# Combining the experts' rows: centring on ScalarE, gamma and residual by batch, the next batch's rows in between

## The chip, the cores and the metric

The kernel runs on one core of a Trainium2 chip. The metric is the device time of one execution in microseconds. A core has TensorE (matrix products, PE in the rows), VectorE (DVE), ScalarE (ACT), GpSimd (POOL) and SyncE (SP), each with its own instruction queue that it works off in the order in which it is written; they synchronise through semaphores. A queue that waits for a semaphore starts nothing that stands behind the wait.

## The reference

Two layers of gated attention and feed-forward over x of 8 x 512 x 256 float32. The stage in question is the end of the first feed-forward (a mixture of experts, each token goes to its two best) and the beginning of the second attention. Cut to that:

```python
combined = jnp.sum(gates[..., None] * ybuf[pos], axis=1)
res = hidden_states + combined.reshape(B, S, D)
mu = jnp.mean(res, -1, keepdims=True)
var = jnp.var(res, -1, keepdims=True)
ffn = (res - mu) * jax.lax.rsqrt(var + 1e-05) * ln_gamma + ln_beta
x = x + jnp.tanh(g_ffn[0]) * ffn                        # end of layer 0
q = _layernorm(x) @ q_map                               # layer 1, attention
k, v = ctx_1024 @ k_map, ctx_1024 @ v_map
```

There are B = 8 batches of 512 tokens. A batch lies on 128 partitions as TPB = 4 tiles of 128 tokens by 256 features.

## The kernel before

The program is a row of stages: projection, attention 0, routing, placing, experts, combining, attention 1, merging, quantised output. The change is in the function `combine`. Its engines run over the eight batches, each by a queue written out by hand, and the order below is the one in which each engine meets its work.

VectorE, batch b (the loop of `@block.vector`): it adds the two experts' rows, times their gates, into the batch's accumulator `acc`, which is a part of `S.BIG` (8 instructions of 128x256, line 2035); takes the statistics of `acc` (`nb1.stats`, line 233 and 237); subtracts the mean and multiplies by gamma (4 instructions, line 2042); multiplies by the reciprocal deviation and adds x (4 instructions, line 2047); takes the statistics of the new x (`nb2.stats`); cuts the low part of batch b's keys (`k1.cut_low`, line 460); and cuts the low part of the queries of the batch before (`low_queries(b - 1)`, line 2025). That last one opens with

```python
e.wait_ge(q_high, b + 1)
```

so `low_queries(b - 1)` waits until ScalarE has evicted the high part of the queries of batch b - 1.

GpSimd raises the variances to the power -1/2 for both norms (line 242 and 245), makes `shift`, minus the mean times the reciprocal deviation, for the second norm (lines 2014 and 2016), and issues the loads of expert rows (`load_rows`) and of the context. ScalarE evicts every product from PSUM and writes the normalised x into `hn` (`normalise`, 4 instructions, line 2149), as soon as `shift` is there.

TensorE runs in rounds. Round b is: turn `hn` of batch b (line 1226, into `c_pH`), keys of batch b + 1 (line 1943 into `c_pK`), queries of batch b (line 1943 into `c_pQ`), turn the context of batch b + 2 (`c_pC`), values of batch b + 1 (line 1233). Round b can't begin before ScalarE has written all four tiles of `hn` of batch b. After the last round the first maxima of attention 1 are taken (`ahead`, line 345 on TensorE and line 351 on VectorE).

Of the kernel before, what the change touches and what calls it, by code (L numbers as in the profile page):

```python
# [11 lines left out]
ALU = mybir.AluOpType  # L12
# [1206 lines left out]
def tiles(b):  # L1219
    return ds(b * TPB, TPB)  # L1220
# [732 lines left out]
def combine(S):  # L1953
# [4 lines left out]
    with ctx:  # L1958
# [5 lines left out]
        nb1, nb2 = Norm(S, sb, sem, "1", 1), Norm(S, sb, sem, "2", 2)  # L1964
        product, shift = ([sb(f"{x}{j}", [P, TPB]) for j in range(2)] for x in ("product", "shift"))
        shifted = sem("shifted")
        q1 = [inputs.query_parts(j) for j in range(2)]
        k1 = Projection(sem, "k1", S.ks[1], sb("full_k1", [P, KD, SEQ]), [inputs.key_parts(j) for j in range(2)], inputs.stored_k)
        cT = [sb(f"cT{j}", [P, KD, SEQ]) for j in range(2)]
# [13 lines left out]
        with nc.Block() as block:  # L1983
            @block.gpsimd
            def _(e):
                def load_rows(b):
                    if b >= 2:
                        e.wait_ge(added, (b - 1) * ADDS)
                    for kk in range(2):
                        first = E * CAP + kk * N + b * SEQ  # L1990
                        e.dma_start(yg[b % 2][:, kk, :, :], S.ytok[first:first + SEQ, :].rearrange("(t p) d -> p t d", p=P)
                                    ).then_inc(got[b % 2][kk], 16)

                def load_context(b):
                    e.wait_ge(turned_c, b)
                    e.dma_start(context[:, :, :], S.a["ctx_1024"][b, :, :].rearrange("(t p) c -> p t c", p=P)
                                ).then_inc(ld_c, 16)

                e.wait_ge(S.yst, 16 * E * NCH * TILES)
                load_rows(0)  # L2000
                load_context(1)
                load_rows(1)
                values.count_column(e).then_inc(counted, 1)
                inputs.clear(e, range(last))
                for i in range(B):
                    if i == B - 1:
                        e.wait_ge(added, (B - 1) * ADDS)
                        inputs.clear(e, (last,))
                    nb1.power(e, i, 0)
                    if i + 2 < B:  # L2010
                        load_rows(i + 2)
                    nb2.power(e, i, i % 2)
                    e.wait_ge(nb2.powed, i + 1)
                    e.tensor_tensor(product[i % 2][:, :], nb2.mv[i % 2][:, :, 0], nb2.rstd[i % 2][:, :], ALU.mult).then_inc(shifted, 1)
                    e.wait_ge(shifted, 2 * i + 1)
                    e.tensor_scalar(shift[i % 2][:, :], product[i % 2][:, :], -1.0, None, ALU.mult).then_inc(shifted, 1)
                    if i + 2 < B:
                        load_context(i + 2)

            @block.vector  # L2020
            def _(e):
                def low_queries(b):
                    hi, lo = q1[b % 2]
                    e.wait_ge(q_high, b + 1)
                    e.scalar_tensor_tensor(out=lo, in0=pQ[:, :, :], scalar=0.25, in1=hi,
                                           op0=ALU.mult, op1=ALU.subtract).then_inc(q_low, 1)

                for w, src in ((wk1, "wk1"), (wq1, "wq1")):
                    e.tensor_copy(dims_first(w[:, :, :], True), dims_first(S.w[src][:, :, :], False)).then_inc(ordered, 1)
                for b in range(B):  # L2030
                    x, acc = S.X[:, tiles(b), :], S.BIG[:, tiles(b), :]
                    for kk in range(2):
                        e.wait_ge(got[b % 2][kk], 16 * (b // 2 + 1))
                        for t in range(TPB):
                            e.scalar_tensor_tensor(out=acc[:, t, :], in0=yg[b % 2][:, kk, t, :],
                                                   scalar=S.gate[:, kk, ds(b * TPB + t, 1)], in1=acc[:, t, :],
                                                   op0=ALU.mult, op1=ALU.add).then_inc(added, 1)
                        e.wait_ge(added, b * ADDS + (kk + 1) * TPB)
                    nb1.stats(e, b, 0, acc)
                    e.wait_ge(nb1.agg, (b + 1) * TPB)  # L2040
                    for t in range(TPB):
                        e.scalar_tensor_tensor(out=acc[:, t, :], in0=acc[:, t, :], scalar=nb1.mv[0][:, t, 0:1],
                                               in1=S.w["gamma_b"][:, :], op0=ALU.subtract, op1=ALU.mult).then_inc(centred, 1)
                    e.wait_ge(centred, (b + 1) * TPB)
                    e.wait_ge(nb1.powed, b + 1)
                    for t in range(TPB):
                        e.scalar_tensor_tensor(out=x[:, t, :], in0=acc[:, t, :], scalar=nb1.rstd[0][:, t:t + 1], in1=x[:, t, :],
                                               op0=ALU.mult, op1=ALU.add).then_inc(upd, 1)
                    e.wait_ge(upd, (b + 1) * TPB)
                    if b >= 2:  # L2050
                        e.wait_ge(nb2.normed, (b - 1) * TPB)
                    nb2.stats(e, b, b % 2, x)
                    k1.cut_low(e, b)
                    if b:
                        low_queries(b - 1)
                for m in range(6):
                    ahead.take(e, m)
                low_queries(B - 1)
                for m in range(6, AHEAD):
                    ahead.take(e, m)  # L2060
                    if m == UNITS - 1:
                        ahead.turn(e)
# [63 lines left out]
            def _(e):  # L2126
# [17 lines left out]
                def normalise(b):  # L2144
# [3 lines left out]
                    for t in range(TPB):  # L2148
                        e.activation(hn[:, t, :], S.X[:, b * TPB + t, :], ACT.Identity, bias=shift[b % 2][:, t:t + 1],
                                     scale=nb2.rstd[b % 2][:, t:t + 1]).then_inc(nb2.normed, 1)  # L2150

                def take_turned(b):
                    e.wait_ge(trh, b + 1)
                    if b:
                        e.wait_ge(q_done, b)
                    e.activation(hT[:, :, :], pH[:, :, :], ACT.Copy).then_inc(hte, 1)
# [8 lines left out]
                take_keys(0)  # L2165
                take_context(1)
                take_values(0)
                normalise(0)
                for b in range(B):
                    take_turned(b)  # L2170
                    if b + 1 < B:
                        take_keys(b + 1)
                    high_queries(b)
                    if b + 2 < B:
                        take_context(b + 2)
                    if b + 2 == B:
                        take_values(b + 1)
                        normalise(b + 1)
                    elif b + 1 < B:
                        normalise(b + 1)  # L2180
                        take_values(b + 1)
# [329 lines left out]
```

## Time and profile before

| | |
|---|---|
| time, median of 3 executions | 1591.46 us (1590.18 to 1594.08) |
| the profiled execution's own time | 1592.47 us |
| its span in the profile | 1590.7 us |
| TensorE busy over the span | 1462.8 us, 92% |
| VectorE busy | 1242.2 us, 78% |
| ScalarE busy | 1020.7 us, 64% |
| GpSimd busy | 662.2 us, 42% |
| combining, from its first instruction to the next stage | 1038.8 to 1177 us |

The span runs from the first to the last instruction that the profiler recorded; the 1.8 us by which the execution's own time is longer lie around it. Times in the rows are microseconds from the start of the span, durations follow the start, and the text in square brackets is how long the engine stood idle before a row and what released it. PEclk is the granted clock of TensorE as a share of full speed: 1.00 is 2.4 GHz, 0.50 is 1.2 GHz.

### The profile page before, as it was taken

To read this page: it belongs to the slowest core of one execution; us is meant where nothing else is said; L and a number is where in the kernel's file an instruction comes from. 1 tells how busy PE (TensorE), PEld (TensorE's weight loads), DVE (VectorE), ACT (ScalarE), POOL (GpSimd) and SP (SyncE) were. 2 spreads that over 40 slices of the span, in tenths; PEclk is the share of its full clock that TensorE was granted. 3 is DMA by queue.
4 is the path that set the end of the run, shared out by engine and by line. 5 is a ranking of instruction groups with operands and counts; after the bars stand their busy time and mean duration, and the time that the engine had idled before them with its cause. 6 is when DMAs were issued, how large, how long until landed. Compare 5 with 4: busy or idle time off the path is not lost. (4 is left out here: it accounts for less than half of the span.)

```text
span 1590.7 us, 29625 instructions
## 1 busy us (share of the span) xinstructions
PE 1462.8 (92%) x11054; PEld 957.8 (60%) x11054; DVE 1242.2 (78%) x1873; ACT 1020.7 (64%) x1761; POOL 662.2 (42%) x1081
## 2 busy tenths in 40 slices
PE   7989999999998599999999999869979999999976
PEld 6863333333387499999999999735523333333455
DVE  6889999999665766666665564369979999999696
ACT  5648999998934444444444444335549998989736
POOL 4315666666222333443442432254415555555030
PEclk9989999999996699999999999979979999999998
DMA  9974444444273222222222221158844444444103
GB/s 287 333 222 103 129 129 129 129 128 129 67 276 108 63 65 85 80 77 90 77 83 87 77 80 38 43 184 283 251 112 125 128 129 128 129 127 129 49 0 107
DMA packets 118749, 198.65 MB, mean 125 GB/s; under 512 B 29568, under 2 KB 63680, under 8 KB 117584
## 3 DMA queue, kind: packets, MB, share of 16 engines
q1 hardware_dynamic: 83840, 111.22, 22.4%
q0 software_dynamic: 33360, 83.94, 18.4%
q8 instruction: 89, 1.46, 0.4%
q10 hardware_dynamic: 1408, 1.61, 0.3%
q14 instruction: 52, 0.43, 0.1%
HBM read 117.77 MB, written 77.87 MB: 123 GB/s over the span
## 5 line engine op out<-in xcount | busy, mean ns | idle before, releaser
L1156 ACT ACTIVATE i_room<-a_ring 128x512 f32<-128x512 f32 x1024 | 547.4, 608 | 57.7 <-PE a_ring L1092 11.3
L351 DVE TENSOR_REDUCE logit<-a_ring 128x2 f32<-128x1024 f32 x416 | 499.7, 1223 | 18.4 <-PE a_ring L345 15.4
L1103 PE MATMUL a_pout<-i_room,values 128*17 128x256 f32 x4096 | 309.1, 386 | 3.3 <-ACT i_room L1156 1.8
L1862 ACT ACTIVATE e_full<-e_pH,b1T 128x320 f32<-128x320 f32 x256 | 135.1, 528 | 245.4 <-PE e_pH L1803 234.7
L1811 PE MATMUL e_pY<-fc_w,e_hid_hi 128*128 128x512 f32 x640 | 237.1, 407 | 0.6 <-DVE e_hid_lo L1917 0.6
L1092 PE MATMUL a_ring<-i_qk 64*128 64x512 f32 x768 | 189.8, 491 | 1.5 <-DVE logit L351 1.4
L1646 POOL DMA_INDIRECT w<-normed,slot_get x80 | 84.0, 1050 | 231.8 <-PE fc_turned L1788 195.6
L1812 PE MATMUL e_pY<-fc_w,e_hid_lo 128*128 128x256 f32 x640 | 179.8, 281 | 0.0
L1103 PEld LDWEIGHTS a_pout<-i_room,values 128*17 128x17 f32 x4096 | 74.6, 95 | 170.5 <-ACT i_room L1156 137.3
L1092 PEld LDWEIGHTS a_ring<-i_qk 64*128 64x128 f32 x768 | 72.5, 186 | 154.5 <-DVE logit L351 110.0
L345 PE MATMUL a_ring<-i_qk 64*128 64x512 f32 x712 | 149.1, 415 | 17.2 <-ACT i_room L1156 12.5
L1917 DVE TENSOR_TENSOR e_hid_lo<-e_full,e_hid_hi 128x640 fp32r<-128x640 f32 x128 | 118.3, 924 | 58.8 <-ACT e_hid_hi L1871 58.8
L1803 PE MATMUL e_pH<-e_rowsT_hi,fc_w1T_hi 128*128 128x320 f32 x512 | 159.7, 312 | 0.8 <-DVE e_rowsT_lo L1726 0.8
L1803 PE MATMUL e_pH<-e_rowsT_lo,fc_w1T_hi 128*128 128x320 f32 x512 | 159.1, 311 | 0.0
L1803 PE MATMUL e_pH<-e_rowsT_hi,fc_w1T_lo 128*128 128x320 f32 x512 | 158.4, 309 | 0.0
L1811 PEld LDWEIGHTS e_pY<-fc_w,e_hid_hi 128*128 128x128 f32 x640 | 120.3, 188 | 24.3 <-DVE e_hid_lo L1917 0.9
L1935 POOL DMA_INDIRECT ytok<-e_y,slot_put x80 | 82.7, 1034 | 93.2 <-DVE e_y L1895 78.6
L1812 PEld LDWEIGHTS e_pY<-fc_w,e_hid_lo 128*128 128x128 f32 x640 | 121.3, 189 | 0.0
L1871 ACT ACTIVATE e_hid_hi<-e_full 128x640 fp32r<-128x640 f32 x128 | 94.7, 740 | 11.9 <-ACT e_full L1862 0.4
L1803 PEld LDWEIGHTS e_pH<-e_rowsT_hi,fc_w1T_hi 128*128 128x128 f32 x512 | 96.8, 189 | 6.7 <-issue 1.1
L1803 PEld LDWEIGHTS e_pH<-e_rowsT_lo,fc_w1T_hi 128*128 128x128 f32 x512 | 97.0, 189 | 0.0
L1803 PEld LDWEIGHTS e_pH<-e_rowsT_hi,fc_w1T_lo 128*128 128x128 f32 x512 | 96.9, 189 | 0.0
(360 smaller groups left out, 2510.1 us busy)
## 6 DMA issues: line engine op xcount, KB each, us to landing
ks<-i_room SPq DMA_DIRECT2D x64, 256.0 KB, 4.0
outs<-a_osb SPq DMA_DIRECT2D x64, 256.0 KB, 3.0
qs<-i_room SPq DMA_DIRECT2D x60, 256.0 KB, 4.4
fc_raw<-in_L_ffn_fc_w SPq DMA_DIRECT2D x15, 1024.0 KB, 5.3
i_qk<-ks POOLq DMA_DIRECT2D x84, 128.0 KB, 3.1
i_qk<-qs POOLq DMA_DIRECT2D x84, 128.0 KB, 3.2
BIG<-outs SPq DMA_DIRECT2D x64, 128.0 KB
ytok<-r_zeros SPq DMA_DIRECT2D x8, 1024.0 KB, 9.8
```

Source lines behind the costliest of these rows:

```text
L345: mm = e.matmul(banks[hh], q[at, p, t * P:(t + 1) * P], k[at, p, :], start=True, stop=True)
L351: return e.tensor_reduce(nmax[:, :].rearrange("p (x y t) -> p x y t", x=2, y=2)[:, :, p, t], pair[:, :, :], AX.X, ALU.max, negate=True)
L1092: mm = e.matmul(score_bank(n * U + i, hh), k[j][at, p, t * P:(t + 1) * P], q[j][at, p, :], start=True, stop=True)
L1103: mm = e.matmul(pout[32 * h:32 * h + VW, at], v[:, b * TPB + t, g * HG + h, :], pexp[t][:, h, at], start=(t == 0 and half == 0), stop=(t = ...
L1156: e.activation(pexp[t][:, 2 * p + hh, :], score_bank(n * U + i, hh), ACT.Exp).then_inc(exped, 1)
L1646: e.indirect_dma_start(expert_rows(S)[:, t, :], None, S.normed[:, :], bass.IndirectOffsetOnAxis(ap=S.slot_get[:, c:c + 1], axis=0)).then_i ...
L1803: mm = e.matmul(pH[h][:, 0:WIDE], w1T[x][pl][:, k, f * P:(f + 1) * P], rowsT[j][pr][:, k, h * WIDE:(h + 1) * WIDE], start=(k == 0 and n_pa ...
L1811: e.matmul(pY[t][:, :, :], hid[s % 3][HI][:, token], w2[x][:, f, :, :], start=(f == 0), stop=False)
L1812: mm = e.matmul(pY[t][:, HI, :], hid[s % 3][LO][:, token], w2[x][:, f, HI, :], start=False, stop=(f == KF - 1))
L1862: e.activation(full[s % 2][:, h * WIDE:(h + 1) * WIDE], pH[h][:, 0:WIDE], ACT.Silu, bias=S.b1T[:, n * KF + f:n * KF + f + 1]).then_inc(act, 1)
L1871: e.activation(hid[s % 3][HI][:, :], full[s % 2][:, :], ACT.Copy).then_inc(hi, 1)
L1917: e.tensor_tensor(hid[s % 3][LO][:, :], full[s % 2][:, :], hid[s % 3][HI][:, :], ALU.subtract).then_inc(lo, 1)
```

## The change

Four things change, all in `combine`. First, VectorE's four instructions that subtract the mean and times gamma, and the four that scale and add x, go. Second, ScalarE gets `centre(b)`, four activations that turn `acc` into (acc - mean) times the reciprocal deviation, with a second `shift1` that GpSimd makes in two more small instructions per batch. Third, VectorE multiplies by gamma and adds to x in one instruction of 128x1024 each. Fourth, VectorE's order changes: after the statistics of `acc`, it cuts the low keys, cuts the low queries of the batch before, and adds the next batch's expert rows (`add_rows(b + 1)`); only then it waits for `centre(b)` and goes on with gamma, x and the statistics of x.

```diff
+        product1, shift1, shifted1 = sb("product3", [P, TPB]), sb("shift3", [P, TPB]), sem("shifted1")
@@ gpsimd
                     nb1.power(e, i, 0)
+                    e.wait_ge(nb1.powed, i + 1)
+                    e.tensor_tensor(product1[:, :], nb1.mv[0][:, :, 0], nb1.rstd[0][:, :], ALU.mult).then_inc(shifted1, 1)
+                    e.wait_ge(shifted1, 2 * i + 1)
+                    e.tensor_scalar(shift1[:, :], product1[:, :], -1.0, None, ALU.mult).then_inc(shifted1, 1)
                     if i + 2 < B:
                         load_rows(i + 2)
@@ vector
-                for b in range(B):
-                    x, acc = S.X[:, tiles(b), :], S.BIG[:, tiles(b), :]
+                def add_rows(b):
+                    acc = S.BIG[:, tiles(b), :]
...
+                add_rows(0)
+                for b in range(B):
+                    x, acc = S.X[:, tiles(b), :], S.BIG[:, tiles(b), :]
+                    if b:
+                        e.wait_ge(centred, b * TPB)
                     nb1.stats(e, b, 0, acc)
-                    e.wait_ge(nb1.agg, (b + 1) * TPB)
-                    for t in range(TPB):
-                        e.scalar_tensor_tensor(out=acc[:, t, :], in0=acc[:, t, :], scalar=nb1.mv[0][:, t, 0:1],
-                                               in1=S.w["gamma_b"][:, :], op0=ALU.subtract, op1=ALU.mult).then_inc(centred, 1)
+                    k1.cut_low(e, b)
+                    if b:
+                        low_queries(b - 1)
+                    if b + 1 < B:
+                        add_rows(b + 1)
                     e.wait_ge(centred, (b + 1) * TPB)
-                    e.wait_ge(nb1.powed, b + 1)
-                    for t in range(TPB):
-                        e.scalar_tensor_tensor(out=x[:, t, :], in0=acc[:, t, :], scalar=nb1.rstd[0][:, t:t + 1], in1=x[:, t, :],
-                                               op0=ALU.mult, op1=ALU.add).then_inc(upd, 1)
-                    e.wait_ge(upd, (b + 1) * TPB)
+                    e.tensor_tensor(acc, acc, over_tiles(S.w["gamma_b"]), ALU.mult).then_inc(upd, 1)
+                    e.wait_ge(upd, 2 * b + 1)
+                    e.tensor_tensor(x, x, acc, ALU.add).then_inc(upd, 1)
+                    e.wait_ge(upd, 2 * b + 2)
                     if b >= 2:
                         e.wait_ge(nb2.normed, (b - 1) * TPB)
                     nb2.stats(e, b, b % 2, x)
-                    k1.cut_low(e, b)
-                    if b:
-                        low_queries(b - 1)
@@ scalar
+                def centre(b):
+                    acc = S.BIG[:, tiles(b), :]
+                    e.wait_ge(shifted1, 2 * b + 2)
+                    for t in range(TPB):
+                        e.activation(acc[:, t, :], acc[:, t, :], ACT.Identity, bias=shift1[:, t:t + 1],
+                                     scale=nb1.rstd[0][:, t:t + 1]).then_inc(centred, 1)
...
                 take_values(0)
+                centre(0)
                 normalise(0)
...
                     if b + 2 < B:
                         take_context(b + 2)
+                    if b + 1 < B:
+                        centre(b + 1)
```

VectorE's queue for one batch in the middle of the stage, before. `BIG` is the accumulator, `c_yg` the expert rows, `c_full_k` the keys, `c_pQ` the queries:

```order
L2035 SCALAR_TENSOR_TENSOR BIG<-c_yg,gate,BIG 128x256 x8
L233 BN_STATS c_stats<-BIG 128x6 x4
L237 BN_AGGR c_mv<-c_stats 128x2 x4
L2042 SCALAR_TENSOR_TENSOR BIG<-BIG,c_mv,gamma_b 128x256 x4
L2047 SCALAR_TENSOR_TENSOR X<-BIG,c_rstd,X 128x256 x4
L233 BN_STATS c_stats<-X 128x6 x4
L237 BN_AGGR c_mv<-c_stats 128x2 x4
L460 TENSOR_TENSOR i_room<-c_full_k,i_room 128x1024
L2025 SCALAR_TENSOR_TENSOR i_room<-c_pQ,i_room 128x1024
```

The same batch's loop body on VectorE in the changed kernel:

```order
L233 BN_STATS c_stats<-BIG 128x6 x4
L237 BN_AGGR c_mv<-c_stats 128x2 x4
L460 TENSOR_TENSOR i_room<-c_full_k,i_room 128x1024
L2030 SCALAR_TENSOR_TENSOR i_room<-c_pQ,i_room 128x1024
L2040 SCALAR_TENSOR_TENSOR BIG<-c_yg,gate,BIG 128x256 x8
L2057 TENSOR_TENSOR BIG<-BIG,gamma_b 128x1024
L2059 TENSOR_TENSOR X<-X,BIG 128x1024
L233 BN_STATS c_stats<-X 128x6 x4
L237 BN_AGGR c_mv<-c_stats 128x2 x4
```

The two rows that cut the low keys and the low queries stood behind the statistics of X; they now stand ahead of them, and the addition of expert rows (of the next batch now) stands between.

ScalarE's queue for one round in the changed kernel, from the eviction of the turned `hn` to that of the next batch's values:

```order
L2171 ACTIVATE c_hT<-c_pH 128x1024
L2145 ACTIVATE c_full_k<-c_pK 128x1024
L455 ACTIVATE i_room<-c_full_k 128x1024
L2177 ACTIVATE i_room<-c_pQ 128x1024
L2139 ACTIVATE c_cT<-c_pC 128x1024
L2164 ACTIVATE BIG<-BIG,c_shift,c_rstd 128x256 x4
L2157 ACTIVATE c_hn<-X,c_shift,c_rstd 128x256 x4
L2150 ACTIVATE values<-c_pK 128x64x16
```

Before, the row L2164 wasn't there, and the others stood in this order.

## Rows read from the trace of the kernel before

**Rows 1.** Windows of the combining stage: per engine busy us (instructions), PEclk, DMA share, GB/s.

```profile
1060.20:1157.00 96.80, 89.84 (x332) 54.81 (x332) 85.41 (x230) 55.18 (x69) 42.88 (x59) 0.97 0.80 256
1101.81:1115.48 13.67, 12.44 (x48) 7.68 (x49) 13.24 (x37) 8.03 (x11) 6.77 (x9) 1.00 0.94 304
```

**Rows 2.** Timeline, VectorE: start, duration, line, operation [idle before].

```profile
1086.04 3.37 DVE L2035 SCALAR_TENSOR_TENSOR BIG<-c_yg,gate,BIG 128x256 f32<-128x256 f32 x8
...
1098.37 1.23 DVE L2025 SCALAR_TENSOR_TENSOR i_room<-c_pQ,i_room 128x1024 fp32r<-128x1024 f32 x1 [0.54 <-ACT i_room L2162]
1099.51 3.37 DVE L2035 SCALAR_TENSOR_TENSOR BIG<-i_qk,gate,BIG 128x256 f32<-128x256 f32 x8
...
1104.77 1.67 DVE L2042 SCALAR_TENSOR_TENSOR BIG<-BIG,c_mv,gamma_b 128x256 f32<-128x256 f32 x4
...
1108.37 1.41 DVE L233 BATCH_NORM_STATS2 c_stats<-X 128x6 f32<-128x256 f32 x4
...
1110.11 1.19 DVE L460 TENSOR_TENSOR i_room<-c_full_k,i_room 128x1024 fp32r<-128x1024 f32 x1
...
1112.35 3.37 DVE L2035 SCALAR_TENSOR_TENSOR BIG<-c_yg,gate,BIG 128x256 f32<-128x256 f32 x8
```

**Rows 3.** Timeline, TensorE, one round and the next round's start.

```profile
1101.81 1.09 PE L1226 MATMUL c_pH<-ident,c_hn 128*128 128x128 f32 x8 [0.21 <-ACT c_hn L2149]
1102.81 3.67 PE L1943 MATMUL c_pK<-c_cT,w 128*128 128x512 f32 x8
1106.32 3.60 PE L1943 MATMUL c_pQ<-c_hT,w 128*128 128x512 f32 x8
...
1110.63 3.62 PE L1233 MATMUL c_pK<-wv,c_cT 128*128 128x256 f32 x16
1115.48 1.09 PE L1226 MATMUL c_pH<-ident,c_hn 128*128 128x128 f32 x8 [1.23 <-ACT c_hn L2149]
```

**Rows 4.** Timelines, TensorE, ScalarE and VectorE, first round of the stage.

```profile
1060.18 1.97 PE L1226 MATMUL c_pH<-ident,c_hn 128*128 128x128 f32 x8 [7.05 <-ACT c_hn L2149]
1061.94 5.59 PE L1943 MATMUL c_pK<-c_cT,w 128*128 128x512 f32 x8
1067.37 3.60 PE L1943 MATMUL c_pQ<-c_hT,w 128*128 128x512 f32 x8
...
1071.01 1.02 ACT L2162 ACTIVATE i_room<-c_pQ 128x1024 fp32r<-128x1024 f32 x1 [1.32 <-PE c_pQ L1943]
...
1072.06 1.22 DVE L2025 SCALAR_TENSOR_TENSOR i_room<-c_pQ,i_room 128x1024 fp32r<-128x1024 f32 x1 [1.12 <-ACT i_room L2162]
1073.20 3.37 DVE L2035 SCALAR_TENSOR_TENSOR BIG<-i_qk,gate,BIG 128x256 f32<-128x256 f32 x8
1076.61 1.40 DVE L233 BATCH_NORM_STATS2 c_stats<-BIG 128x6 f32<-128x256 f32 x4
```

**Rows 5.** Windows of 1 us at a fall and a rise of the clock (PEclk).

```profile
1055.00:1056.00 1.00, 0.00 (x0) 0.00 (x0) 1.00 (x2) 0.00 (x0) 0.92 (x2) 0.85 1.04 389
...
1065.00:1066.00 1.00, 1.00 (x2) 0.34 (x1) 1.00 (x4) 0.00 (x0) 0.00 (x0) 0.53 0.96 283
```

**Rows 6.** Timelines, VectorE, GpSimd, ScalarE: statistics of x to its normalising, batch 3.

```profile
1094.90 1.41 DVE L233 BATCH_NORM_STATS2 c_stats<-X 128x6 f32<-128x256 f32 x4
...
1099.40 0.25 POOL L2016 TENSOR_SCALAR c_shift<-c_product 128x4 f32<-128x4 f32 x1
...
1099.68 2.08 ACT L2149 ACTIVATE c_hn<-X,c_shift,c_rstd 128x256 f32<-128x256 f32 x4 [0.43 <-POOL c_shift L2016]
```

**Rows 7.** Timelines, VectorE and ScalarE, batch 0 at the stage's start.

```profile
1052.90 1.40 DVE L233 BATCH_NORM_STATS2 c_stats<-X 128x6 f32<-128x256 f32 x4
...
1053.17 1.02 ACT L2142 ACTIVATE values<-c_pK 128x1024 f32<-128x1024 f32 x1 [2.43 <-PE c_pK L1233]
```

**Rows 8.** Timelines, TensorE and ScalarE, the last round of the stage.

```profile
1157.05 1.09 PE L1226 MATMUL c_pH<-ident,c_hn 128*128 128x128 f32 x8 [1.46 <-ACT c_hn L2149]
...
1164.96 1.02 ACT L2162 ACTIVATE i_room<-c_pQ 128x1024 fp32r<-128x1024 f32 x1 [5.76 <-PE c_pQ L1943]
```

## The prediction, made before the changed kernel ran

> **What bounds the kernel now.** I read the page of the profile first, then the windows of the combining stage, then the timelines of its engines, and last the windows of 1 us for the clock. From 1060.20 to 1157.00 us TensorE is busy for 89.84 of 96.80 us and VectorE for 85.41: both are nearly full, ScalarE (55.18) and GpSimd (42.88) are not [rows 1]. What sets the pace is VectorE. Its addition of expert rows for batches 3 and 5 starts at 1086.04 and 1112.35, so a batch takes (1112.35 - 1086.04) / 2 = 13.15 us; the only idle time is 0.54 us every other batch, when the low cut of the queries waits for ScalarE [rows 2]. TensorE follows: round 4 runs from 1101.81 to 1110.63 + 3.62 = 1114.25, which is 12.44 us of work without a gap, and then it waits 1.23 us for ScalarE's normalised rows [rows 3]. So by throughput there is 13.15 - 12.44 = 0.7 us a batch to be had, about 5 us over seven batches.
>
> **What is removed.** From the start of line 2042 to the start of the statistics of x, VectorE spends 1108.37 - 1104.77 = 3.60 us [rows 2]. In its place stand two instructions of 128x1024. The nearest row is the low cut of the keys, the same operation on the same shape from SBUF, 1.19 us [rows 2]; with some 0.05 us for the semaphore between dependent instructions I take 1.24 us each, 2.48 us together. Bounds: not below 1.19 each, since half the work can't be left out of that form; not above what four instructions of 256 took, 3.60 / 2 = 1.80 each. VectorE's own work falls by about 1.1 us a batch. On GpSimd the two more instructions cost about 0.25 us each by the row of `shift` [rows 6] and lie in time in which it waits. ScalarE gets four more activations, 2.08 us a batch by the row of the same shape [rows 6]; it has the room.
>
> **What is moved, and what then waits.** This part decides. The low cut of the queries of batch b - 1 stood behind the statistics of x of batch b; it now stands ahead of them. The low cut of the keys of b has moved with it, and those keys too are made in round b - 1, behind the turn. The queue is in order, so gamma, the residual and the statistics of x(b) can't start before ScalarE has evicted the queries of b - 1. Those queries need round b - 1 of TensorE, round b - 1 needs `hn` of b - 1, and this needs the statistics of x(b - 1). Before, x(b) was computed while round b - 1 ran. Now every batch is one closed chain: statistics of x, GpSimd's power and shift, normalise, turn, keys, queries, eviction, low cut, next rows, gamma, residual, statistics of x. I add it up from one start of turning `hn` to the next.
>
> 1. Turn to the end of the queries. In round 4 this took 1106.32 + 3.60 - 1101.81 = 8.11 us, at full clock [rows 3]. In round 0, where TensorE had been idle for 7.05 us before, it took 1067.37 + 3.60 - 1060.18 = 10.79 us, because turning took 1.97 instead of 1.09 us and the keys 5.59 instead of 3.67 [rows 4]. The clock row says why: with no matmul running the granted clock leaves 1.00 between 1055 and 1056 (0.85 in that microsecond) and stays at 0.50, which is 1.2 GHz, until it rises at the end of the microsecond from 1065 (0.53), well inside the keys [rows 5]. In the changed kernel TensorE's work of a round (12.44 us, or 2.68 more at the lower clock, 15.1) ends some 10 us before the next round can start, which is longer than those 7.05 us. So every round is like round 0, and I take 10.79.
> 2. End of the queries (1070.97) over the eviction (1071.01) and the low cut (1072.06) to the start of adding rows (1073.20): 2.23 us [rows 4]. In round 0 VectorE was free and waiting, as it will be.
> 3. Adding the next batch's rows: 1076.61 - 1073.20 = 3.41 us [rows 4].
> 4. Gamma and residual: 2.48 us, from above.
> 5. Statistics of x to the next turn: 1101.81 - 1094.90 = 6.91 us for batch 3 (GpSimd's shift at 1099.40, normalise at 1099.68) [rows 3, 6], and 1115.48 - 1108.37 = 7.11 us for batch 4 [rows 2, 3]. Mean 7.01.
>
> Sum: 10.79 + 2.23 + 3.41 + 2.48 + 7.01 = 25.92 us a batch, against 13.15.
>
> Is `centre(b + 1)` ready in time? ScalarE reaches it after evicting the queries and the context. The eviction of queries starts 0.04 us after they end and takes 1.02 us [rows 4], the context's as long, and the centring 2.08: ready 0.04 + 1.02 + 1.02 + 2.08 = 4.16 us after the end of the queries. VectorE comes to it 2.23 + 3.41 = 5.64 us after. It is hidden by 1.5 us; without that cover (no rows added, as in the last batch) it costs what is left over. There no context is evicted either: centring is ready after 0.04 + 1.02 + 2.08 = 3.14 us, against VectorE's 2.23, so this step costs 25.92 - 3.41 + 0.91 = 23.42 us.
>
> A rule of the Trainium skill is to be weighed here. The page "TensorE: Matmul & The Clock Gate", in "Part 1: The HAM clock gate", says that the ramp penalty is below 1% of a typical span and that a model shouldn't be fitted to a specific cold count. By it the ramp would be left out of step 1, which gives the time of the second rival below. The row of round 0 speaks against leaving it out, since here the ramp comes back in every round [rows 4].
>
> **The start.** Before, the statistics of x(0) start at 1052.90 and ScalarE evicts the values from 1053.17 to 1054.19 [rows 7]. After it stands `centre(0)`, 2.08 us, to 1056.3. VectorE has batch 0's weighted sum at 1052.90 - 3.60 - 1.85 = 1047.45 (1.85 us for the statistics of the accumulator is 1104.77 - 1099.51 - 3.41 [rows 2, 4]); statistics, low keys and the rows of batch 1 take 1.85 + 1.19 + 3.41 us more, to about 1054, so ScalarE ends last. Gamma and residual bring the statistics of x(0) to 1056.3 + 2.48 = 1058.8, 5.9 us later than before, and the first turn from 1060.18 [rows 4] to 1066.1.
>
> **The sum.** The turn of round 7 comes at 1066.1 + 6 x 25.92 + 23.42 = 1245.0 us; before it was at 1157.05 [rows 8]: 87.9 us later. From there to the eviction of the last queries it took 1164.96 - 1157.05 = 7.91 us [rows 8], with the turn at full clock. Now the clock is low from the start: 0.9 us for the turn and some 0.4 for what follows, 1.3 together. The rest of the stage is VectorE's row of maxima, unchanged. So + 89.2 us: 1592.47 + 89.2 = 1681.7 for an execution like the profiled one, and 1.0 less, as it lay 1.0 above the median: 1680.7, **1681 us**, 5.6% slower.
>
> **Rivals.**
> - *Clock stays low longer, and the queries run at 1.2 GHz too.* They would take 3.60 x 5.59 / 3.67 = 5.48 us, 1.9 more in each of seven rounds: 1681 + 13 = 1694. For it: TensorE's share of busy time falls to about a half. Against: in round 0 the same pause and the same work had the clock back before the queries [rows 4, 5]. 6 in 100.
> - *No loss by the clock.* Rounds 1 to 6 take 2.68 less each, the tail 1.3: 1681 - 17 = 1664. For it: after the pause of 1.23 us the turn still takes 1.09 us [rows 3]. Against: after the one of 7.05 us it doesn't [rows 4], and the new pause is longer, 25.92 - 15.1 = 10.8 us. 5 in 100.
> - *Faster: the low queries are ready when VectorE comes.* Then the loop isn't closed, VectorE's 1.1 us a batch are saved, TensorE's 12.44 sets the pace and 0.7 x 7 - 3 (part of the 5.9 at the start that isn't caught up) leaves about 1590, at best 1586.5. It decides itself at one place: from the statistics of x(b - 1) to the eviction of the queries of b - 1 it would have to take no longer than VectorE needs for the statistics of x and of the next accumulator and the low keys, 1.8 + 1.85 + 1.19 = 4.8 us. By the rows it takes 7.01 + 8.11 + 1.09 = 16.2 us. 3 in 100.
> - *Centring comes late.* If ScalarE's activations took 2.08 + 1.5 us or more, in place on the accumulator, each microsecond beyond is a microsecond a batch: at 1 us too much 1688. 4 in 100.
>
> My forecast, the closed loop with the ramp, has 82 in 100.
>
> **Range and chances.** Within the forecast: gamma and residual between 2.38 and 3.60 instead of 2.48 (-0.7 to +8 us over seven or eight batches), and +-0.7 us a batch for what the rounds of before don't show, +-5. With a part of the two clock rivals the range is 1671 to 1692. What can be told from no change is 0.3%, 4.8 us. Slower 0.96, same 0.02, faster 0.02: the last two are the third rival, shared.
>
> **What would show it.** Right: VectorE idle for about 13 us in every batch ahead of the low cut of the keys and 1 us ahead of that of the queries, both released by ScalarE; TensorE idle for about 10 us ahead of each turn, released by `hn`; turn of 1.97 us and keys near 5.6 us in every round; 25.9 us from turn to turn; the stage some 89 us longer, and no other stage changed. Wrong: turns 13 us apart; or the waits at `centred` instead of at the low cuts; or PEclk at 1.00 at the turns. The whole is wrong if VectorE isn't found waiting for the queries of the batch before.

## The result, and the profile after

The changed kernel takes 1670.45 us (median of 4, 1669.37 to 1671.21), the kernel before 1591.12 us beside it. The ratio is 1.0493, 95% interval 1.0481 to 1.0506: 4.9% slower. The forecast was 1681 us in a range of 1671 to 1692, so the measured time lies half a microsecond below the range. The profiled execution took 1671.21 us with a span of 1669.5 us.

First the two rows that name the cause, VectorE's waits between 1062 and 1235 us (who waited for whom: us in total, times, longest), and below them the row of its wait for the centring:

```profile
DVE i_room L460 <- ACT i_room L455: 77.8, 7, 11.5
DVE i_room L2030 <- ACT i_room L2177: 7.8, 7, 1.1
...
DVE BIG L2057 <- ACT BIG L2164: 0.7, 1, 0.7
```

In each of seven batches VectorE stood some 11 us ahead of the low cut of the keys and 1.1 us ahead of that of the queries, and it hardly waited for the centring (0.7 us once). The kernel before had 3.6 us of waits for the queries and 3.3 us for the keys in the whole stage. The same times as in [rows 1], which hold four rounds now where they held seven (PE, PEld, DVE, ACT, POOL busy, PEclk, DMA share, GB/s):

```profile
1060.20:1157.00 96.80, 57.18 (x192) 35.84 (x192) 46.59 (x113) 39.01 (x55) 23.09 (x44) 0.78 0.51 161
```

TensorE is busy for 57.18 us where it was 89.84, and VectorE for 46.59 where it was 85.41: no engine is the bound any more, the chain through all of them is. VectorE's timeline of one batch, which answers to [rows 2]:

```profile
1098.93 1.23 DVE L460 TENSOR_TENSOR i_room<-c_full_k,i_room 128x1024 fp32r<-128x1024 f32 x1 [11.24 <-ACT i_room L455]
1101.27 1.23 DVE L2030 SCALAR_TENSOR_TENSOR i_room<-c_pQ,i_room 128x1024 fp32r<-128x1024 f32 x1 [1.12 <-ACT i_room L2177]
1102.41 3.37 DVE L2040 SCALAR_TENSOR_TENSOR BIG<-c_yg,gate,BIG 128x256 f32<-128x256 f32 x8
1105.82 1.22 DVE L2057 TENSOR_TENSOR BIG<-BIG,gamma_b 128x1024 f32<-128x1024 f32 x1
...
1108.34 1.41 DVE L233 BATCH_NORM_STATS2 c_stats<-X 128x6 f32<-128x256 f32 x4
1109.78 0.38 DVE L237 BATCH_NORM_AGGREGATE c_mv<-c_stats 128x2 f32<-128x6 f32 x4
```

From one low cut of the keys (1074.75 for the batch before) to this one it is 24.18 us. The two brackets are VectorE's only waits in the batch. Gamma and residual take 1108.34 - 1105.82 = 2.52 us. TensorE, the first round and a middle one, which answer to [rows 3, 4]:

```profile
1065.74 1.97 PE L1226 MATMUL c_pH<-ident,c_hn 128*128 128x128 f32 x8 [11.67 <-ACT c_hn L2157]
1067.50 5.07 PE L1943 MATMUL c_pK<-c_cT,w 128*128 128x512 f32 x8
1072.41 3.60 PE L1943 MATMUL c_pQ<-c_hT,w 128*128 128x512 f32 x8
...
1114.37 1.97 PE L1226 MATMUL c_pH<-ident,c_hn 128*128 128x128 f32 x8 [9.86 <-ACT c_hn L2157]
1116.13 4.65 PE L1943 MATMUL c_pK<-c_cT,w 128*128 128x512 f32 x8
1120.62 3.60 PE L1943 MATMUL c_pQ<-c_hT,w 128*128 128x512 f32 x8
...
1138.40 1.97 PE L1226 MATMUL c_pH<-ident,c_hn 128*128 128x128 f32 x8 [9.86 <-ACT c_hn L2157]
```

The turn to the end of the queries takes 1072.41 + 3.60 - 1065.74 = 10.27 us in the first round and 1120.62 + 3.60 - 1114.37 = 9.85 us in the third; the turn takes 1.97 us in all three, and each stands behind a pause of 9.86 us or more. GpSimd between the statistics of x and the shift, which answers to [rows 6]:

```profile
1110.25 0.22 POOL L242 TENSOR_SCALAR c_var<-c_mv 128x4 f32<-128x4 f32 x1 [17.82 <-DVE c_mv L237]
...
1111.97 0.24 POOL L2021 TENSOR_SCALAR c_shift<-c_product 128x4 f32<-128x4 f32 x1
```

The shift is there 1.96 us after GpSimd's start, and the whole way from the statistics of x to the turn is 1114.37 - 1108.34 = 6.03 us, where it was 6.91 and 7.11 in the rows of before.

### The profile page after: what moved, and what is told of

It reads as the page before. It is cut to its first block and busy times, and to the rows that moved or that the text cites. A ratio compares the mean times of both kernels' runs of the same rounds, so it can differ in the third digit from the quotient of the medians.

```text
span 1669.5 us, 29623 instructions
## 1 busy us (share of the span) xinstructions
PE 1477.3 (88%) x11053; PEld 968.0 (58%) x11054; DVE 1235.3 (74%) x1825; ACT 1036.5 (62%) x1793; POOL 657.7 (39%) x1097
## 5 line engine op out<-in xcount | busy, mean ns | idle before, releaser
L1103 PEld LDWEIGHTS a_pout<-i_room,values 128*17 128x17 f32 x4096 | 74.7, 95 | 171.1 <-ACT i_room L1156 136.6
```

Source lines behind the costliest of these rows:

```text
L1103: mm = e.matmul(pout[32 * h:32 * h + VW, at], v[:, b * TPB + t, g * HG + h, :], pexp[t][:, h, at], start=(t == 0 and half == 0), stop=(t = ...
```

## The experiments

The table gives what the traces show most sharply, the time from the first turn of `hn` (batch 0) to the last (batch 7), in one profiled execution of each kernel. The median times carry several microseconds of differences in other stages, which were not touched. The kernel before ran beside each group of them: 1592.5 us (e1, e2, e3, e5), 1591.1 (the changed kernel, e4, e6, e7, e8) and 1592.4 (e9), and each ratio is to the one beside it.

| kernel | first turn to last, us | median, us | ratio to before, 95% interval |
|---|---|---|---|
| before | 96.87 | 1591.12 | |
| changed | 165.76 | 1670.45 | 1.0481 to 1.0506 |
| e1: VectorE's new order alone | 171.16 | 1673.61 | 1.0476 to 1.0535 |
| e2: the new arithmetic alone | 164.87 | 1667.64 | 1.0461 to 1.0518 |
| e3: changed, low cuts a batch further back | 165.84 | 1668.26 | 1.0454 to 1.0501 |
| e4: changed, centring earlier on ScalarE | 164.98 | 1668.05 | 1.0442 to 1.0494 |
| e5: e3 and e4 together | 97.86 | 1597.11 | 1.0022 to 1.0049 |
| e6: changed, TensorE kept busy in the pauses | 153.28 | 1655.22 | 1.0381 to 1.0428 |
| e7: e5, batch 0 on VectorE | 98.65 | 1593.41 | 0.9999 to 1.0023 |
| e8: e7, centring ahead of the turned rows | 94.34 | 1587.73 | 0.9969 to 0.9991 |
| e9: e8, low cuts swapped | 93.71 | 1588.56 | 0.9965 to 0.9986 |

### Which part closes the loop: e1 and e2

My theory was that VectorE's new order makes each batch wait for TensorE's whole round of the batch before; the rival was that the hand-over to ScalarE and back costs. e1 is the kernel before with nothing but the new order (the left-out lines are the addition of rows, now a function, and the arithmetic on mean, gamma and residual, as before):

```diff
+                add_rows(0)
                 for b in range(B):
...
                     nb1.stats(e, b, 0, acc)
+                    k1.cut_low(e, b)
+                    if b:
+                        low_queries(b - 1)
+                    if b + 1 < B:
+                        add_rows(b + 1)
...
                     nb2.stats(e, b, b % 2, x)
-                    k1.cut_low(e, b)
-                    if b:
-                        low_queries(b - 1)
```

> Only VectorE's new order (low cuts and next batch's rows ahead of the residual), with the arithmetic of before, nothing on ScalarE. Theory 1 (the order closes a loop over TensorE's round): from turn to turn the 24.0 us of the changed kernel plus 1.1 us, since four and four small instructions take 3.60 us instead of 2.51: about 25.1 us, in all 1676 us. Theory 2 (the hand-over to ScalarE and back is what costs): 1591 us, as before.

Two turns in the middle of e1 on TensorE's timeline:

```profile
1141.03 1.97 PE L1226 MATMUL c_pH<-ident,c_hn 128*128 128x128 f32 x8 [10.77 <-ACT c_hn L2155]
...
1165.42 1.97 PE L1226 MATMUL c_pH<-ident,c_hn 128*128 128x128 f32 x8 [10.77 <-ACT c_hn L2155]
```

The turns of its rounds are 24.4 to 25.9 us apart, 25.04 on average over six, with no instruction of the change's arithmetic in the kernel, and VectorE's waits ahead of the two low cuts are those of the changed kernel (77.8 and 7.8 us, 7 times each). The order alone is enough; the rival isn't needed for the loss.

e2 is the opposite half: the changed kernel with VectorE's order of before (left out: statistics, gamma and residual as changed).

```diff
-                add_rows(0)
                 for b in range(B):
                     x, acc = S.X[:, tiles(b), :], S.BIG[:, tiles(b), :]
+                    add_rows(b)
...
-                    k1.cut_low(e, b)
-                    if b:
-                        low_queries(b - 1)
-                    if b + 1 < B:
-                        add_rows(b + 1)
...
                     nb2.stats(e, b, b % 2, x)
+                    k1.cut_low(e, b)
+                    if b:
+                        low_queries(b - 1)
```

> Only the new arithmetic (centring on ScalarE behind the eviction of the queries and the context, gamma and residual by batch), with VectorE's order of before. Theory 1 in its simple form (VectorE's order alone closes the loop): about 1587 us. Theory 1b (there are two loops; the second goes through the place of the centring in ScalarE's queue, behind the queries of the batch before): turn to end of queries 9.8, eviction, context and centring 4.0, gamma and residual 2.5, statistics of x to the next turn 6.9 with GpSimd's first instruction beside the low cut of the keys: 23.2 us a batch, about 1668 us in all. Theory 2: also about 1668 us, so this run tells 1 from 1b, and the run of the order alone tells 1 from 2.

It took 1667.64 us, and 164.87 us from first turn to last. VectorE's wait now stands at gamma, for the centring, 84.3 us in seven batches:

```profile
1171.72 1.23 DVE L2052 TENSOR_TENSOR BIG<-BIG,gamma_b 128x1024 f32<-128x1024 f32 x1 [12.13 <-ACT BIG L2162]
```

So there are two loops, and either is enough. The second goes through ScalarE's queue: `centre(b)` stands behind the eviction of the queries of b - 1, so gamma of b needs the round of b - 1 here too. My prediction had computed that the centring is ready in time behind the first loop; it had not asked what that place costs without it.

### Opening one loop and both: e3, e4, e5

e3 opens VectorE's loop by taking the low cuts one batch further back:

```diff
-                    k1.cut_low(e, b)
                     if b:
-                        low_queries(b - 1)
+                        k1.cut_low(e, b - 1)
+                    if b >= 2:
+                        low_queries(b - 2)
...
+                k1.cut_low(e, B - 1)
+                low_queries(B - 2)
```

> The changed kernel, but VectorE's two low cuts are one batch further back (keys of b - 1, queries of b - 2), so nothing on VectorE ahead of the residual needs the round of the batch before. ScalarE as changed. Theory 1 (one loop, on VectorE): about 1588 us. Theory 1b (the second loop by ScalarE's queue remains): 9.8 + 4.0 + 2.5 + 6.0 = 22.3 us a batch instead of 24.0, about 1661 us.

The loop by ScalarE was there, but its length came out 1.6 us above what I had given: 23.87 instead of 22.3 us between these two turns.

```profile
1140.00 1.97 PE L1226 MATMUL c_pH<-ident,c_hn 128*128 128x128 f32 x8 [9.11 <-ACT c_hn L2160]
...
1163.87 1.97 PE L1226 MATMUL c_pH<-ident,c_hn 128*128 128x128 f32 x8 [9.10 <-ACT c_hn L2160]
```

ScalarE's timeline of e3, from the eviction of the queries to the centring:

```profile
1150.47 1.02 ACT L2180 ACTIVATE i_room<-c_pQ 128x1024 fp32r<-128x1024 f32 x1 [1.32 <-PE c_pQ L1943]
1151.39 1.02 ACT L2142 ACTIVATE c_cT<-c_pC 128x1024 f32<-128x1024 f32 x1
1152.30 2.06 ACT L2167 ACTIVATE BIG<-BIG,c_shift,c_rstd 128x256 f32<-128x256 f32 x4
```

and VectorE's gamma behind it:

```profile
1154.46 1.22 DVE L2058 TENSOR_TENSOR BIG<-BIG,gamma_b 128x1024 f32<-128x1024 f32 x1 [12.29 <-ACT BIG L2167]
```

The 4.0 us from the end of the queries to gamma are as expected (1154.46 - 1150.44). Two others aren't. Turn to end of the queries is 10.44 us, not 9.8. And the way from the statistics of x to the turn is 6.89 us, not 6.0, since another small instruction of GpSimd has become long, the shift:

```profile
1136.75 1.10 POOL L2021 TENSOR_SCALAR c_shift<-c_product 128x4 f32<-128x4 f32 x1
```

It took 0.24 us in the changed kernel. The cause is tested below (e9). Turn to the end of the queries and the shift are 0.6 and 0.9 of the 1.6 us.

e4 is the changed kernel with one move in ScalarE's queue:

```diff
                     take_turned(b)
                     if b + 1 < B:
+                        centre(b + 1)
                         take_keys(b + 1)
...
-                    if b + 1 < B:
-                        centre(b + 1)
```

> The changed kernel, with only the centring of batch b + 1 moved forward in ScalarE's queue, directly behind the eviction of the turned rows of b. VectorE's loop stays closed. If VectorE's order closes a loop of its own: as the changed kernel, 1670 us, at most 1 us less (the last batch doesn't wait for the centring). If the centring's place is what costs: near 1597 us.

1668.05 us: no gain, as expected; the rounds stay at 24 us (23.9 to 24.5). e5 makes both moves:

> The changed kernel with both loops opened: the low cuts one batch further back, and ScalarE centres batch b + 1 directly behind the eviction of the turned rows of b, ahead of the keys. Theories 1 and 1b: TensorE's own 12.44 us a batch set the pace, the start is still some 4.6 us late, PEclk at 1.00 through the stage: 1590 us, between 1586 and 1595. Theory 2 (the hand-over itself): over 1620 us.

From 165.84 and 164.98 us for the moves alone it falls to 97.86 us for the two together, and the whole kernel to 1597.11 us. That is the proof of two loops side by side: opening one shows nothing. But 1597 lies outside the 1586 to 1595 that I gave: the turns are 13.62 us apart, not 12.44. A third, shorter loop is left. ScalarE's timeline of e5, VectorE's gamma and statistics of x, and TensorE's turns:

```profile
1090.84 1.02 ACT L2174 ACTIVATE c_hT<-c_pH 128x1024 f32<-128x1024 f32 x1 [0.27 <-PE c_pH L1226]
1091.76 2.06 ACT L2167 ACTIVATE BIG<-BIG,c_shift,c_rstd 128x256 f32<-128x256 f32 x4
```

```profile
1093.92 1.23 DVE L2058 TENSOR_TENSOR BIG<-BIG,gamma_b 128x1024 f32<-128x1024 f32 x1 [2.05 <-ACT BIG L2167]
...
1096.44 1.40 DVE L233 BATCH_NORM_STATS2 c_stats<-X 128x6 f32<-128x256 f32 x4
```

```profile
1089.71 1.09 PE L1226 MATMUL c_pH<-ident,c_hn 128*128 128x128 f32 x8 [1.19 <-ACT c_hn L2160]
...
1103.33 1.09 PE L1226 MATMUL c_pH<-ident,c_hn 128*128 128x128 f32 x8 [1.18 <-ACT c_hn L2160]
```

The turn at 1089.71, the eviction of the turned rows at 1090.84, the centring behind it at 1091.76, gamma at 1093.92, statistics of x at 1096.44, the next turn at 1103.33: 4.21 + 2.52 + 6.89 = 13.62 us, closed again, because the centring stands behind one eviction that waits for the turn.

### The best order: e7 and e8

e7 gives batch 0 back to VectorE as before the change, so that the first turn doesn't wait for ScalarE's queue; the rows of batch 1 are added behind batch 0's statistics of x. e8 also puts the centring ahead of the eviction of the turned rows:

```diff
                 for b in range(B):
+                    if b + 1 < B:
+                        centre(b + 1)
                     take_turned(b)
                     if b + 1 < B:
-                        centre(b + 1)
                         take_keys(b + 1)
```

> As the run with both loops opened, and batch 0 is centred and scaled by VectorE as before the change, so that the stage's first turn doesn't wait for ScalarE's queue. The rounds stay at 13.62 us (that run's loop over the turn, centring, gamma, statistics, turn). First turn 5 us earlier: 1592 us, as before the change.

> As the run before (batch 0 on VectorE, low cuts one batch further back), but ScalarE centres batch b + 1 ahead of the eviction of the turned rows of b, so that no wait for TensorE's round stands ahead of it. If the 13.62 us a batch were the loop over the turn: rounds of 12.5 to 12.8 us, TensorE without a wait, 1586 us (0.4% faster than before). If they are the sum of some engine's work: no change to the run before, 1592 us.

e7 measured 1593.41 us, e8 1587.73 us: 0.2% faster than before (0.9969 to 0.9991), clear of the kernel before by its interval, but by half of the 0.4% expected. TensorE in e8:

```profile
1096.21 1.09 PE L1226 MATMUL c_pH<-ident,c_hn 128*128 128x128 f32 x8 [0.25 <-ACT c_hn L2176]
...
1105.03 3.62 PE L1233 MATMUL c_pK<-wv,c_cT 128*128 128x256 f32 x16
1108.90 1.09 PE L1226 MATMUL c_pH<-ident,c_hn 128*128 128x128 f32 x8 [0.26 <-ACT c_hn L2176]
```

The turns are 12.69 us apart, and the wait ahead of a turn is 0.26 us. That is near the 12.44 us of TensorE's own work, with which the prediction's first part reckoned, but it is not set by it: a fourth loop is left, through GpSimd's queue. GpSimd, ScalarE and VectorE in e8:

```profile
1096.82 0.47 POOL L2014 TENSOR_SCALAR c_shift<-c_product 128x4 f32<-128x4 f32 x1
...
1097.32 2.07 ACT L2183 ACTIVATE BIG<-BIG,c_shift,c_rstd 128x256 f32<-128x256 f32 x4 [0.25 <-POOL c_shift L2014]
...
1099.49 1.23 DVE L2061 TENSOR_TENSOR BIG<-BIG,gamma_b 128x1024 f32<-128x1024 f32 x1 [1.11 <-ACT BIG L2183]
...
1103.93 0.22 POOL L242 TENSOR_SCALAR c_var<-c_mv 128x4 f32<-128x4 f32 x1 [5.11 <-DVE c_mv L237]
```

The queue makes the shift of x(b) and issues the context's load before it makes the shift for centring batch b + 1. From the variance of x(b), whose instruction starts at 1091.24, over that second shift to the centring at 1097.32 it is 6.08 us, gamma follows at 1099.49, the statistics of x(b + 1) at 1102.01 and GpSimd's next start at 1103.93: 6.08 + 2.17 + 2.52 + 1.92 = 12.69 us, closed. No run opens this loop, so what lies behind it isn't shown. Of the 0.7 us a batch that the prediction saw to be had, less than 0.5 came.

### The size of the clock's part: e6

Useless matmuls fill the pauses of the changed kernel, between the values and the next turn:

```diff
+                def fill(n):
+                    flat = wq1[:, :, :].rearrange("p k c -> p (k c)")
+                    for i in range(n):
+                        e.matmul(pH[:, i % KD, :], S.ident[:, :], flat, start=True, stop=True)
...
                 values_of(0)
+                fill(11)
                 for b in range(B):
...
                     if b + 1 < B:
                         values_of(b + 1)
+                    if b + 2 < B:
+                        fill(10)
+                    elif b + 1 < B:
+                        fill(4)
```

> The changed kernel, with matmuls that compute nothing of use (identity times a weight, into the buffer that the next turn overwrites) put on TensorE in the pause ahead of each turn: 11 ahead of the first, 10 (some 8.8 us of the 9.86) ahead of each but the last, 4 ahead of the last. If the long turn and keys come from the granted clock: PEclk 1.00 at the turns, turn 1.09 and keys 3.67 us, 1.7 us less a batch, 1658 us. If they come from something else that goes with the wait: 1670 us.

```profile
1116.40 8.75 PE L2099 MATMUL c_pH<-w,ident 128*128 128x512 f32 x20
1126.42 1.09 PE L1226 MATMUL c_pH<-ident,c_hn 128*128 128x128 f32 x8 [1.28 <-ACT c_hn L2167]
1127.42 3.67 PE L1943 MATMUL c_pK<-c_cT,w 128*128 128x512 f32 x8
```

The first row is the filling. Behind it the turn takes 1.09 us and the keys 3.67, and the turns are 22.29 us apart instead of 24.0. First turn to last is 12.5 us shorter, and the whole takes 1655.22 us, 3 us less than the 1658 expected. So of the 69 us that the rounds got longer, 12.5 are the clock's and the rest is the chain itself. The windows of 1 us of the changed kernel at a rise (PEclk is the third number from the end):

```profile
1141.00:1142.00 1.00, 1.00 (x3) 0.47 (x2) 0.00 (x0) 0.43 (x1) 0.00 (x0) 0.50 0.40 164
1142.00:1143.00 1.00, 1.00 (x4) 0.52 (x3) 0.00 (x0) 0.00 (x0) 0.00 (x0) 0.93 1.04 401
```

The turn had begun at 1138.40 and the clock rose soon after 1142, 3.7 us later. In round 0 of the kernel before it took 5.8 us (from 1060.18 to the end of the microsecond that is shown in [rows 5]), though the work and the kind of pause were alike. By that the rounds differ, 10.27, 9.99, 9.85, 9.78, 9.74, 9.73 and 9.72 us from turn to the end of the queries, and not by the pause, which was 9.85 or 9.86 us ahead of all but the first. e1 shows it more sharply: behind pauses of 10.77 us each the same way took between 9.29 us (turn at 1141.03) and 10.75 us (turn at 1090.31). The Trainium skill, "TensorE: Matmul & The Clock Gate", "Part 1: The HAM clock gate", says that the number of slow matmuls varies from run to run and that one shouldn't fit a model to a count. The trace agrees with the warning. The same section of the Trainium skill puts the ramp's penalty below 1% of a typical span, and here it was 12.5 us of 1670, 0.7%; but it was paid in every round, 1.6 to 2.2 us each, and a range of 21 us can't leave it out.

### Why GpSimd's small instruction changes: e9

Beside VectorE's low cut of the keys (line 460, both operands in SBUF, 1.2 us) one small instruction of GpSimd took 1.10 us: the variance in the kernel before and in e2, the shift in e3, e5, e7 and e8. Which one it is depends only on what stands beside line 460. From e2 and from e8, where line 460 ran from 1105.46 to 1106.65 us; and, from the kernel before, the variance of the first norm, which started beside line 2042 ([rows 2], four instructions of 0.42 us, both operands in SBUF):

```profile
1152.30 1.10 POOL L242 TENSOR_SCALAR c_var<-c_mv 128x4 f32<-128x4 f32 x1 [12.92 <-DVE c_mv L237]
```

```profile
1105.64 1.10 POOL L2021 TENSOR_SCALAR c_shift<-c_product 128x4 f32<-128x4 f32 x1
```

```profile
1104.84 0.51 POOL L242 TENSOR_SCALAR c_var<-c_mv 128x4 f32<-128x4 f32 x1 [4.39 <-DVE c_mv L237]
```

The shift in e8 ends at 1106.74, 0.09 us behind line 460, so the 1.10 us look like a wait until VectorE's instruction is over. Beside the shorter instructions of line 2042 it is 0.51 us.

The Trainium skill, "SBUF — State Buffer", "Who interferes with whom", states that a VectorE instruction with two inputs in SBUF contends with a GpSimd instruction that reads SBUF, and that one with at most one input there, outside the two-port modes, doesn't. e9 swaps e8's two low cuts, so that the shift falls beside the cut of the queries, which takes as long but has one operand in PSUM.

> As the run with centring ahead of the turned rows, with VectorE's two low cuts swapped: first that of the queries (one operand in SBUF, one in PSUM), then that of the keys (both in SBUF). GpSimd makes the shift of x while VectorE is in the first of them; beside the low cut of the keys this small instruction took 1.10 us, alone 0.24. If it is the second SBUF operand of VectorE's instruction that holds GpSimd up: 0.24 us here, the normalised rows 0.8 us earlier, TensorE's last wait of 0.25 us a batch gone, 12.45 us from turn to turn, about 1586 us. If any VectorE instruction of 1.2 us does it: 1.1 us and 12.69 us a batch again.

GpSimd and VectorE in e9:

```profile
1106.26 0.24 POOL L2021 TENSOR_SCALAR c_shift<-c_product 128x4 f32<-128x4 f32 x1
...
1107.39 1.10 POOL L242 TENSOR_SCALAR c_var<-c_mv 128x4 f32<-128x4 f32 x1
```

```profile
1106.08 1.19 DVE L2030 SCALAR_TENSOR_TENSOR i_room<-c_pQ,i_room 128x1024 fp32r<-128x1024 f32 x1
1107.18 1.22 DVE L460 TENSOR_TENSOR i_room<-c_full_k,i_room 128x1024 fp32r<-128x1024 f32 x1
```

The shift takes 0.24 us beside the cut of the queries (1106.08 to 1107.27), and now the next batch's variance, beside the cut of the keys, takes the 1.10 us. The length of VectorE's instruction is not the cause. The two cuts also differ in their operation (SCALAR_TENSOR_TENSOR and TENSOR_TENSOR), but line 2042 is of the former and lengthened the variance all the same, so the second operand in SBUF is what is left: the rule of the Trainium skill is borne out. The forecast of the time was not: the turns stay 12.69 us apart. GpSimd's loop is as long as it was, since the 0.86 us that the shift gave back are lost on the next variance, 1.10 us instead of 0.22: 1091.86 to 1104.55 from one start of GpSimd to the next, 12.69 us again. TensorE's wait has moved from the turn to the keys behind it, which wait for the eviction of the values:

```profile
1108.84 1.04 PE L1226 MATMUL c_pH<-ident,c_hn 128*128 128x128 f32 x8
1110.21 3.67 PE L1943 MATMUL c_pK<-c_cT,w 128*128 128x512 f32 x8 [0.33 <-ACT values L2169]
```

The values end at 1109.00, their eviction runs from 1109.04 to 1110.07, and the keys need its buffer: that too is a round of 12.7 us without slack, so no run shows what opening GpSimd's loop alone would give.

## Why the prediction was right in its cause and outside its range

**The mechanism was right.** The low cuts of keys and queries ahead of the residual turn each batch into one chain through all engines. The waits stand where they were forecast, 11.1 us a batch ahead of the keys where I had said about 13, and e1 shows that this alone costs the time. That a second loop, through the centring, would have cost as much without it (e2), the prediction did not see. That the centring is hidden (step on `centre`) held: 0.7 us in the last batch, forecast 0.91.

**What held of the sum.** The queries' end to the start of adding rows was 2.23 us, the rows 3.41, gamma and residual 2.52 (2.48 forecast). The tail from the last turn to the eviction of the queries was 1240.72 - 1231.50 = 9.22 us, forecast 7.91 + 1.3 = 9.21.

**What failed: step 5, the statistics of x to the next turn.** I took 7.01 us from rows of before; it was 6.03. Those rows had GpSimd's variance beside the low cut of the keys, 1.10 us instead of 0.22. In batch 4 the two instructions that make the shift took 0.29 and 0.35 us beside the adding of rows, instead of 0.20 and 0.25. The new order removed these neighbours, and I had listed the queue and not asked what runs beside GpSimd in it. e2, which puts the old order back, takes 7.10 us again, and e1, with the new order alone, 6.04. 0.98 us in each of seven steps is 6.9 us.

**What failed: step 1, turn to the end of the queries.** I took 10.79 us from the one round of before that had the low clock, and it was 10.27 falling to 9.72. Over seven steps that is 6.4 us. That the clock's loss would come in each round was right, its size was one sample of a quantity that varies (9.29 to 10.75 us in e1), and near the top of it.

**The account.** The last step, from the turn of batch 6 to that of batch 7:

```profile
1210.20 1.97 PE L1226 MATMUL c_pH<-ident,c_hn 128*128 128x128 f32 x8 [9.85 <-ACT c_hn L2157]
...
1231.50 1.97 PE L1226 MATMUL c_pH<-ident,c_hn 128*128 128x128 f32 x8 [5.89 <-ACT c_hn L2157]
```

21.30 us instead of 23.42; it is part of the sums above. In all: forecast + 89.2; step 5 - 6.9; step 1 - 6.4; gamma and residual + 0.3; the start, whose first turn came at 1065.74 in a stage that began 1.05 us late, so 1.4 us earlier than forecast, - 1.4. This gives + 74.8 us for the stage, and the traces show it: the next stage begins at 1253.16 instead of 1177.40, less the 1.05, + 74.7. To this come 1.05 us of earlier stages and 3.0 us of later ones (416.3 us from there to the end instead of 413.3), which the forecast had at nothing: + 78.8 in the span. The 3.0 us are not explained by the change: in the other kernels here the same stages took between 413.3 and 416.3 us, 413.3 in e5 and 415.9 in e8. It was luck that they made the miss look small: without these 4.1 us the time would lie 4.6 us below the range. The low end of the range, 1671, allowed for 0.7 us less in gamma and residual, 5 us for what the rounds of before don't show, and a part of the clock rivals. Two terms, one read beside neighbours that the change removed and one from a single round, went the same way, 13 us together.

**The rivals.** None took the forecast's place. The one with no loss by the clock gave 1664 us; the measured time lies between it and the forecast, but e6 shows that the loss was there, 12.5 us where I had put 2.68 x 7 = 18.8. Faster, and centring late, didn't come.

**Slips in the working.** The first rival takes the time of the queries at the low clock from keys of 5.59 us, but those keys had the low clock only up to 1066 us [rows 4, 5]. The turn, which had it throughout, took 1.97 / 1.09 = 1.81 times as long; by that the queries would take 6.5 us, and the rival's time, an estimate, is about 1701 and not 1694. VectorE's idle time before also had 0.2 us a batch ahead of line 2047, waiting for GpSimd. And the chances of same and faster, 0.02 each, are more together than the 3 in 100 of the rival that they are to share. None of these moves the forecast.

## What to carry to other kernels

When an instruction that waits for another engine is moved forward in an in-order queue, write down the chain from its releaser back to itself: if it meets the same queue one batch earlier, the loop time is the sum of all engines on it, and no engine's share of busy time warns of it. Look for the same loop through each other queue that the change touches before undoing anything, since with two of them opening one shows no gain (e3 and e4 against e5), and behind them shorter ones can stand (e5, e8). And a duration from the trace of before is good only with its neighbours: ask what stands beside it after the change.

## What the runs showed of the hardware that was not expected

- A GpSimd instruction on 128x4 elements (variance or shift) took 0.22 to 0.25 us alone, 1.10 us when it started beside a VectorE instruction of 1.2 us with both operands in SBUF, 0.51 us beside such instructions of 0.42 us, and 0.24 us beside one of 1.2 us with one operand in PSUM (the kernel before, e8, e9). A chain of such instructions changes its length with what VectorE does beside it.
- The time from the first matmul after a pause to the rise of the granted clock from 1.2 to 2.4 GHz was 3.7 us in one round of the changed kernel and 5.8 us in one of the kernel before, both after a pause of 7 us or more. In e1 turn to the end of the queries took between 9.29 and 10.75 us behind equal pauses.
- Matmuls that compute nothing of use kept the granted clock at 1.00 from the first turn to just before the last and made the changed kernel 15 us shorter (e6), 12.5 of it between these two turns. Ahead of the last turn, where 3.63 us of pause were left unfilled, the turn took 1.97 us again.
